# Three loads moved behind stores in the opening, and seven loads moved behind the reciprocals in the last batch, of an attention and feed-forward kernel

## The reference

```python
q = (layernorm(x) @ W_q.T)   # split into 16 heads of 32
k = (ctx @ W_k.T)
v = (ctx @ W_v.T)
scores = einsum('bhqd,bhkd->bhqk', q, k) / sqrt(32)
attn = exp(clip(scores, -50, 50)); attn = attn / sum(attn)
x = x + (attn @ v) @ W_o.T * mask
# feed forward: int8 quantised layernorm(x) times int8 quantised rhs, scaled back
x = x + int8_matmul(layernorm(x), rhs)
```

## Time and profile before

| what | value |
|---|---|
| median of 3 runs (lowest, highest) | 1716.47 us (1715.9, 1716.8) |
| the profiled execution, its own time | 1714.59 us |
| its span, first to last instruction | 1712.8 us |
| PE busy | 1673.7 us, 98% |
| PE weight load busy | 1012.2 us, 59% |
| DVE busy | 1489.9 us, 87% |
| ACT busy | 1315.1 us, 77% |
| POOL busy | 133.8 us, 8% |
| SP's DMA queue | 287.64 MB, 65.8% of the 16 engines |

### The profile page before, as it was taken

One profiled execution on the slowest core, in us unless ns is written; L12 is line 12 of the kernel. 1 busy time (PEld: TensorE's weight loads), 2 busy tenths in 40 slices (PEclk: granted clock), 3 DMA queues, 4 the chain that ended last, 5 costly groups with the idle time before them and its releaser, 6 DMA issues.

```text
span 1712.8 us, 29863 instructions
## 1 busy us (share of the span) xinstructions
PE 1673.7 (98%) x10418; PEld 1012.2 (59%) x10448; DVE 1489.9 (87%) x1705; ACT 1315.1 (77%) x1730; POOL 133.8 (8%) x75
## 2 busy tenths in 40 slices
PE   7999999999999999999999999999999989999998
PEld 7996565656565665656656566666656434444445
DVE  4657888888988989999898998989899799999997
ACT  4557887888877877877787787777878778788875
POOL 0000000000001111011110101111011000000001
PEclk8999999999999999999999999999999999999999
DMA  7677556666566566756657576566855878988971
GB/s 258 203 227 203 132 145 157 162 168 172 130 168 174 139 179 165 200 137 170 173 134 202 130 199 153 153 181 155 209 130 146 207 169 211 218 177 201 215 173 62
DMA packets 235060, 294.87 MB, mean 172 GB/s; under 512 B 28184, under 2 KB 142360, under 8 KB 234392
## 3 DMA queue, kind: packets, MB, share of 16 engines
q1 hardware_dynamic: 231688, 287.64, 65.8%
q10 hardware_dynamic: 3216, 5.24, 1.1%
HBM read 201.07 MB, written 91.48 MB: 171 GB/s over the span
## 4 chain that ended last, share of the span: by engine, by line
PE 82%; ACT 6%; DVE 5%; DMA 3%; issue 2%; SPq 1%; POOL 0%; POOLq 0%; DVEq 0%; ACTq 0%
PE wsum L999 25%; PE tile L962 24%; PE scores L984 21%; ACT probs L1247 5%; PE scores L1148 3%; PE scores L962 3%; DVE acc L1552 3%; PE tile L1031 1%; PE tile L1148 1%; DMA o_parts<-sums 1%; DMA row_lo<-o_parts 1%; PE tile L1111 1%; PE tile L1088 1%; PE tile L569 1%; PE scores L626 1%
## 5 line engine op out<-in xcount | busy, mean ns | idle before, releaser
L1247 ACT ACTIVATE probs<-scores 128x1024 f32<-128x1024 f32 x939 | 914.7, 1026 | 206.6 <-PE scores L984 169.4
L1552 DVE TENSOR_TENSOR acc<-acc,probs 128x2048 f32<-128x2048 f32 x439 | 1003.5, 2286 | 40.3 <-ACT probs L1247 25.8
L999 PE MATMUL wsum<-probs,v_sb 128*32 128x512 f32 x4096 | 492.5, 598 | 0.0
L984 PE MATMUL scores<-q_stack,k_stack 128*128 128x512 f32 x1536 | 444.6, 410 | 2.5 <-ACT probs L1247 1.7
L984 PEld LDWEIGHTS scores<-q_stack,k_stack 128*128 128x128 f32 x1536 | 265.1, 188 | 212.9 <-ACT probs L1247 121.6
L999 PEld LDWEIGHTS wsum<-probs,v_sb 128*32 128x32 f32 x4096 | 107.3, 109 | 243.6 <-issue 229.7
L1654 POOL TENSOR_TENSOR rstd<-var_eps,minus_half 128x1 f32<-128x1 f32 x48 | 106.0, 2208 | 1190.4 <-DVE var_eps L1446 1190.4
L1552 DVE TENSOR_TENSOR acc<-probs 128x2048 f32<-128x2048 f32 x32 | 73.4, 2293 | 57.6 <-PE tile L1031 52.7
L1148 PE MATMUL scores<-q_stack,k_stack 128*128 128x512 f32 x342 | 110.8, 425 | 10.3 <-ACT probs L1247 10.3
L962 PE MATMUL tile<-ctx_hi,wk_hi 128*128 128x256 f32 x412 | 116.6, 283 | 0.0
L962 PE MATMUL tile<-ctx_hi,wk_lo 128*128 128x256 f32 x412 | 116.1, 282 | 0.0
(11 more groups left out here) (255 smaller groups left out, 1964.8 us busy)
## 6 DMA issues: line engine op xcount, KB each, us to landing
k_stack<-k_parts SPq DMA_DIRECT2D x312, 256.0 KB, 7.6
q_stack<-q_parts SPq DMA_DIRECT2D x124, 256.0 KB, 7.3
v_sb<-v_parts SPq DMA_DIRECT2D x80, 256.0 KB, 7.5
v_parts<-v_stage SPq DMA_DIRECT2D x64, 256.0 KB, 5.1
raw<-ctxT SPq DMA_DIRECT2D x27, 512.0 KB, 5.7
k_parts<-stage_hi SPq DMA_DIRECT2D x96, 128.0 KB, 4.7
k_parts<-stage_lo SPq DMA_DIRECT2D x96, 128.0 KB, 2.5
x_in<-x SPq DMA_DIRECT2D x33, 256.0 KB, 4.9
```

The lines of the kernel that those rows point to most:

```text
L984: last = nc.tensor.matmul(scores[:, h, :], k_stack[:, kt // 4, h, (kt % 4) * P:(kt % 4 + 1) * P], q_stack[:, qb, h, :], start=True, stop=True)
L999: last = nc.tensor.matmul(wsum[DH * h:DH * h + DH, :], v_sb[:, kt, DH * h:DH * h + DH], probs[:, n % RING, h, :], start=(kt == 0), stop=(k ...
L1247: nc.scalar.activation(probs[:, slot % RING, 2 * pair:2 * pair + 2, :], score_banks(seg, slot, pair), ACT.Exp, scale=1.0 / math.sqrt(DH)). ...
L1552: nc.vector.tensor_tensor(acc[:, :, :], other, probs[:, slot % RING, :, :], ALU.add).then_inc(sems["add_done"], 1)
```

## The change

Three edits, all in SyncE's order of issue; no other engine's instructions change.

- In segment 0 the loads of the output weights, the feed-forward weights and the mask go from slot 8 to slot 12.
- In the last batch's first half (`i` = 0) the load of the rows goes from slot 1 to slot 5, the load of keys 1536 to 2047 from step 2 to step 5, the load of values 1536 to 2047 from step 3 to step 5. `chain`, which stands first in each slot, therefore issues the two transfers of the reciprocals ahead of them. The waits of these loads go with them.
- The condition for `i` = 5 is only written differently: step 5 for the keys, as before.

```diff
-                    if step == (5 if slot > KT and c == 2 else 2):
+                    if slot == 5 and c == 0:
+                        load_o_rows(sp, 0, slice(0, G), slice(P, QB), "rows_loaded5")
+                    if step == (5 if i in (0, 2 * 2 + 1) else 2):
                         if i == 0:
                             all_parts_stored(ct, "v_stored")
                         ct.wait_alone(sp, "scores_full", 2 * KT * half)
                         load_k(sp, j, 3)
-                    if slot == 1 and c == 0:
-                        load_o_rows(sp, 0, slice(0, G), slice(P, QB), "rows_loaded5")
...
-                    if step == 3:
+                    if step == (5 if i == 0 else 3):
                         ct.wait_alone(sp, "step_summed", KT * half)
                         load_v(j, 3)
...
-                    if seg.s == 0 and slot == 8:
+                    if seg.s == 0 and slot == 12:
                         load_weight("o", woT)
                         load_last()
```

## The result

The changed kernel takes 1706.1 us in the median of four runs (1705.3 to 1707.4); the kernel before, run beside it, 1716.4 (1715.9 to 1716.8). The ratio is 0.994 [0.993, 0.995]: 10.3 us, 0.6%, faster. The forecast was 13.5 us, 1703.0; the time lies inside its range, on the side of the smaller gain. The profiled execution took 1705.6 us by its own time.

What follows compares the result with a forecast made beforehand. TensorE, with 82% of the chain, was taken as the bound, and DVE in the last batch's first half. Gains of 6.5 + 2.05 + 5.0 = 13.5 us from the median 1716.47 gave 1703.0 us, range 1701.0 to 1708.5.

Steps and rivals of the forecast that it cites:

- The value store, 27.8: Opening: the first value store, issued at 25.28 where the weights were, lands at 27.8 us.
- the slow matmuls' 2.05 us: Opening: if the clock stays full over the shorter pause, the 21 slow query matmuls gain 2.05 us.
- the 6.5: Opening: ACT's second value copy, and with it the first query matmul, comes 6.5 us earlier.
- 8.55: The opening's whole gain in us: the earlier first query matmul plus query matmuls at full clock.
- The weights now stand ahead of the query stores … Cost 0: Opening: ACT may wait up to 1.6 us for a query store, but TensorE's seven banks cover it; cost 0.
- The last batch's gain of 5.0: Last batch, first half: DVE's 5.13 us wait for the reciprocals goes; 5.0 us gained after 0.1 us cost.
- 1 us for the reciprocals: Last batch: time allowed for the reciprocals ahead of the rows, which land at 1358.2 with 3.6 us to spare.
- Rival 4: Last batch: rows come too late for row tile 1 on TensorE; slower by over 0.2%, chance 0.02.
- The slide of the queries, 1.9 us: Last batch: the next half's queries land 1.9 us later, at 1377.2; cost 0.1 us, upper end 2 or more.
- Rival 1: Last batch: next half's queries slide 4.0 us, giving back part of the gain; 1704.2 to 1706.1 us, chance 0.17.
- Rival 2: Opening: clock stays at 1.2 GHz over the shorter pause, losing 2.05 us; 1705.1 us, chance 0.10.
- Rival 3: Last batch: reciprocals' load takes over 9.6 us, landing after 1359.1; all lost at 14.7 us; 1707.9 us, chance 0.07.

Runs made afterwards that it cites:

- e3_behind_q: The changed kernel with the weights in slot 15 of segment 0, behind the first query stores, in place of slot 12: 1702.9 us, ratio 0.991.
- e6_half: The changed kernel with the output weights in slot 12 but the feed-forward weights and the mask in slot 15: 1702.7 us, ratio 0.992.
- e1_opening: Against the kernel before, only the opening's edit (weights in slot 12), the last batch as before: 1708.5 us, ratio 0.995.
- e2_last: Against the kernel before, only the last batch's edit, the weights in slot 8 as before: 1711.7 us, ratio 0.997.
- r1_changed: The changed kernel itself, unchanged, measured again beside three variants on one chip: 1707.3 us, ratio 0.995.
- e7_probe_after: The changed kernel with DVE's product one addition (two slots) earlier in the last batch's first half, rows behind the reciprocals' load: 1707.7 us.
- e4_rows_first: The changed kernel with only the last batch's row load back in slot 1, ahead of the reciprocals: 1703.0 us, ratio 0.991.
- the probes: Two kernels with DVE's product one addition earlier in the last batch's first half, rows behind the reciprocals' load or ahead of it: 1707.7 and 1707.8 us.

## Why the prediction was right, and where it was not

- **The value store, 27.8: right.** It landed at 27.2, 2.53 us after its issue; the first query matmul came at 29.81 (forecast 30.3), the idle time 0.67 us (1.2). The clock held, so the slow matmuls' 2.05 us came too: 9.0 us by 34 to 43 us, against 6.5 + 2.05. Of the 7.03 us at the first query matmul some 0.7 were there before the edit's place, so 6.3 are the edit's, near the 6.5: the close match of the place is right, that of the full 9.0 with 8.55 is in part luck.
- **"The weights now stand ahead of the query stores … Cost 0": the step that failed.** Two parts of it. The store was sized as the value store before, 7.4 us, to land at 40.5; it took 9.16 and landed at 42.4, and ACT waited 3.20 us and not up to 1.6. And the cover was counted on the wrong path. Seven banks do cover TensorE's own query tiles; but DVE works in program order, and its squares of the key tile, which wait for ACT's, stand ahead of the scaling of the next rows (L1467). So TensorE ran out not of banks but of rows: 0.22 + 1.70 us idle, and up to 1.5 us lost to the half clock where it came. In the forecast's own terms the cost is 3.9 us in the profiled execution and not 0. e3_behind_q and e6_half, which leave 0 or 1 MB ahead of the first query stores, have neither.
- **The last batch's gain of 5.0: right in its mechanism; its size is not settled.** DVE's wait went whole, the reciprocals' store took 1.4 us. Against the trace before the gain is 4.6 us, 3.4 to 4.8 in the others with this order; but the 5.13 us that the sum rests on are of one execution, and e1_opening waits 3.17 us at the same place in the same order. Against that trace the changed kernel's gain is 2.6. e2_last, 5.1 us by its medians, can't tell these apart.
- **"1 us for the reciprocals" ahead of the rows: mis-sized.** The spread load takes 6.6 to 7.1 us. The rows landed at 1358.0, 13.1 us after that load's issue, where the step had 8.7. Of the 3.6 us to spare nothing was left (TensorE took them at 1358.07), and five of the traces with the rows behind wait there for 0.4 to 1.2 us (r1_changed the longest). Rival 4's place was the right one to watch; its price was far off.
- **The slide of the queries, 1.9 us: mis-sized.** They landed at 1374.2; moved back by the 4.64 us that all is early, that is 1378.8, against 1375.3 before: 3.6 us. Rival 1 had 4.0, and in part it came true: a pause of 1.5 to 2.3 us in all six traces with the rows behind and the product in its place, and of 0.8 in e7_probe_after. The queue runs empty, share 0.02 over 1340 to 1346, while SP waits for the reciprocals and their store. That with the rows ahead the queries are in time, in all four kernels, shows that this idle time counts; but its length, 6 us, was forecast right, and why 3.6 us of slide came of it and not 1.9 stays open.
- **Rival 2** did not come where it was placed, at 29.8, but did at 47 us, which the forecast had no pause for. **Rival 3** did not come: the load was in time by DVE's timeline.
- **The sum.** Forecast 8.55 + 5.0. The profiled execution: 9.0 at first, less 2.3 for the rows and 1.6 for the clock, less 1.1 at 523 us, 0.9 back later, and 4.6 in the last batch; that is 9.5, and the trace has 9.2 at L1031, the rest being small shifts. The 1.1 and the 0.9 are loads whose landing scatters; the 3.9 us in the opening are the step that failed, and 2.3 of them did not hang on the clock. That 10.3 us came out is also the luck of the run: the same kernel measured again (r1_changed) gained 7.3, little more than half of the forecast.

## What to carry to other kernels

A bulk load that is moved from ahead of one store goes ahead of the next: look at who is stuck while that store waits, through the in-order program of every engine between it and the bound, not only through the buffers of the bound engine. And while an issuing engine waits for a small round trip, keep something in its queue that is wanted soon after: here the rows, ahead of the reciprocals, cost their store up to 1.0 us (0.2 in e4_rows_first), for which nothing waited, and made the last half 0.4 to 1.8 us shorter.

## What the runs showed that was not expected

- A 256 KB load that spreads 8 KB over 128 partitions (`denoms<-recip_row`) takes 6.6 and 7.1 us in the probes, 5.8 to 8.3 wherever DVE waits for it, each time with other loads behind it; while it alone moves data the DMA share is 0.26. A 256 KB value store takes 2.5 us.
- A 128 KB store right behind 2 MB of loads lands after 9.2 us, behind 1 MB after 6.1, with no bulk load ahead after 2.2.
- The same pause of 1.70 us, at the same instruction, was followed by 3.4 us of half clock in one execution (1.53 us lost) and by none in another.
